# First cross attention: four passes of eight batches turned into one run over 32 batches

## What is computed

```python
def _L0_xattn_ref(x, context, Wq, Wk, Wv, Wo, bo):      # x (32,128,128), context (32,77,96)
    q = (x @ Wq).reshape(B, S, 8, 64).transpose(0, 2, 1, 3)
    k = (context @ Wk).reshape(B, 77, 8, 64).transpose(0, 2, 1, 3)
    v = (context @ Wv).reshape(B, 77, 8, 64).transpose(0, 2, 1, 3)
    attn = softmax(einsum('bhsd,bhld->bhsl', q, k) * 64 ** -0.5)
    out = einsum('bhsl,bhld->bhsd', attn, v)
    return out.transpose(0, 2, 1, 3).reshape(B, S, 512) @ Wo + bo
...
x = _layernorm(x + _L0_xattn_ref(x, ctx_768, ...), axis=-1)
```

## Time and profile before

| | us |
|---|---|
| runs shown | 3458.25, 3458.6, 3462.52 |
| median | 3458.6 |
| the profiled execution | 3463.82 |
| its span | 3462.0 |
| first cross attention in it, to the next stage's first instruction | 269.45 (7.8% of the span) |

### The profile page before, as it was taken

The page is one execution under the profiler, slowest core; times in us unless marked ns, Lnnn a source line. Parts: engine busy times, 40 slices in busy tenths (PEclk is TensorE's granted clock), DMA queues, the critical chain, the costliest instruction groups (busy, mean ns, idle before and its releaser), DMA issues. The chain is left out here.

```text
span 3462.0 us, 84257 instructions
## 1 busy us (share of the span) xinstructions
PE 2679.9 (77%) x31931; PEld 1923.7 (56%) x31931; DVE 2379.6 (69%) x7057; ACT 1979.8 (57%) x3723; POOL 1688.9 (49%) x1265
## 2 busy tenths in 40 slices
PE   1899999888857678889799999866655657858846
PEld 1677777656647565566355555544333447845546
DVE  6678778756557878956667766559973544568945
ACT  1688888644436746755555555555423724556747
POOL 3788888422257615510356656613321257805544
PEclk9999999899958887999999999977768858978958
DMA  4333333221112301000000000000007012301013
GB/s 136 63 63 61 60 62 62 43 95 51 51 40 75 97 1 69 2 1 1 1 3 2 3 3 2 3 1 19 25 22 231 7 46 66 92 15 38 2 34 102
DMA packets 103292, 151.42 MB, mean 44 GB/s; under 512 B 26266, under 2 KB 76524, under 8 KB 101756
## 3 DMA queue, kind: packets, MB, share of 16 engines
q1 hardware_dynamic: 91418, 122.93, 14.3%
q0 software_dynamic: 10912, 22.70, 2.0%
q10 hardware_dynamic: 562, 0.41, 0.1%
HBM read 81.20 MB, written 49.04 MB: 38 GB/s over the span
## 5 line engine op out<-in xcount | busy, mean ns | idle before, releaser
L551 DVE TENSOR_REDUCE MX<-banks 128x8 f32<-128x1152 f32 x128 | 173.8, 1358 | 97.4 <-PE banks L320 97.3
L2550 POOL TENSOR_TENSOR SM<-SM,RZ 128x1232 f32<-128x1232 f32 x64 | 144.0, 2250 | 160.3 <-DVE RZ L2592 160.3
L1810 POOL DMA_INDIRECT sorted_rows<-SRC,IDX x160 | 156.8, 980 | 131.8 <-DVE IDX L1939 85.1
L1823 POOL DMA_INDIRECT expert_results<-Y,DST x181 | 178.4, 986 | 81.1 <-DVE DST L2006 34.4
L1592 PE MATMUL banks<-XC,WR 128*128 128x128 f32 x1448 | 197.7, 281 | 0.5 <-ACT XC L1712 0.4
L514 POOL TENSOR_TENSOR FL<-FL,sb_f_sin 128x1024 f32<-128x1024 f32 x60 | 142.3, 2371 | 83.3 <-DMA FL<-RAW 83.2
L1592 PEld LDWEIGHTS banks<-XC,WR 128*128 128x128 f32 x1448 | 181.1, 197 | 2.7 <-ACT XC L1712 2.1
L2889 POOL TENSOR_TENSOR KQ<-T,EX 128x1024 f32<-128x1024 f32 x32 | 76.2, 2381 | 209.2 <-ACT EX L2870 209.2
L555 DVE TENSOR_TENSOR SM<-banks,MX 128x512 f32<-128x512 f32 x256 | 168.2, 678 | 0.0
L461 ACT COPY PT<-banks 128x1024 f32<-128x1024 f32 x128 | 128.4, 1004 | 54.3 <-PE banks L346 54.3
L2518 ACT COPY PT<-banks 128x1024 f32<-128x1024 f32 x128 | 129.0, 1008 | 48.4 <-PE banks L2439 47.6
(11 more groups left out here) (579 smaller groups left out, 8774.7 us busy)
## 6 DMA issues: line engine op xcount, KB each, us to landing
FL<-RAW SPq DMA_DIRECT2D x508, 64.0 KB, 2.3
sorted_rows<-in_zeros_dram SPq DMA_DIRECT2D x33, 528.0 KB, 8.2
XR<-sorted_rows SPq DMA_DIRECT2D x181, 66.0 KB, 1.9
SRC<-expert_results SPq DMA_DIRECT2D x16, 512.0 KB, 6.9
T<-s4d_k_dram SPq DMA_DIRECT2D x8, 1024.0 KB, 10.4
weight_region<-in_l_ffn__wall_dram SPq DMA_DIRECT2D x1, 4112.0 KB
film_dram<-F SPq DMA_DIRECT2D x8, 512.0 KB, 2.9
FO<-film_dram SPq DMA_DIRECT2D x8, 512.0 KB, 4.2
```

Source lines behind the costliest of these rows:

```text
L551: nc.vector.tensor_reduce(MX[:, n % 2], sc, AXX, ALU.max).then_inc(s.mx, 1)
L1810: nc.gpsimd.indirect_dma_start(out=rows, out_offset=bass.IndirectOffsetOnAxis(ap=IDX[:, k, t:t + 1], axis=0), in_=SRC[:, t, k, :], in_offs ...
L1823: nc.gpsimd.indirect_dma_start(out=results, out_offset=bass.IndirectOffsetOnAxis(ap=DST[:, j % ST:j % ST + 1], axis=0), in_=Y[:, j % ST, : ...
L2550: nc.gpsimd.tensor_tensor(SM[:, t % 4], SM[:, t % 4], bc(RZ[:, t % 2, :].unsqueeze(2), [P, H, L]), ALU.mult).then_inc(s.nm, 1)
```

## The change

`l0_xattn` becomes one run over `NB` = 32 batches in eight groups of four; `decoder` calls it once, with all transfers in one list. In detail:

- The projections of group 0 for `x`, keys and queries stand ahead of the loop; its values, and the units of every later group, are spread over the steps of the group before (`SLOTS`: three places in each step, 13 units a group). They use two banks (2 and 3) in turn. A unit waits until the unit two places ahead has been copied out. ACT copies `x`, the queries and two of four values, DVE the keys and the other values.
- `XT`, `QT`, `KT`, `VA` hold two groups instead of eight batches.
- Scores: eight matmuls of 64 rows and 77 columns instead of four of 128 rows and 154 columns; the keys lose their zeros and the clearing. Even heads go to bank 0, odd heads to bank 1. There is one pair of banks instead of two, so that the scores of a batch wait for the subtraction of the batch before.
- The weights are turned by halves: 16 transposes of 64 rows instead of 8 of 128, into two banks, and ACT copies them once instead of twice. `SM` has 51 more columns so that each transpose is 128 wide.
- The layer norm is taken for each batch, by the logarithm and the exponential on ACT (three short instructions), a product on DVE, and scale and shift on ACT, four and more steps behind the batch. No table is changed in the loop.
- POOL adds the bias to four batches at a time, in place, and no longer clears the weights.
- `E.r` and `E.xt` go.

```diff
-    proj = [("k", g, j) for g in range(NG) for j in range(NJ)] + [("q", g, j) for g in range(NG) for j in range(NJ)] + \
-           [("v", t, 0) for t in range(NB)]
+    NB = B_ALL
+    GROUP = ["X", "K0", "K1", "K2", "K3", "Q0", "Q1", "Q2", "Q3", "V0", "V1", "V2", "V3"]
+    SLOTS = [[["X"], ["K0", "K1"], ["K2"]], [["K3"], ["Q0"], ["Q1"]], [["Q2"], ["Q3"], ["V0"]], [["V1"], ["V2"], ["V3"]]]
+    def due(i, slot):
...
+        new = [(item, i // GB + 1) for item in SLOTS[i % GB][slot]] if i // GB + 1 < NG else []
+        first = [[("V0", 0), ("V1", 0)], [("V2", 0)], [("V3", 0)]][slot] if i == 0 else []
+        return first + new
...
             def _(pe):
+                def produce(item, g):
+                    k = place[item, g]
+                    if k >= 2:
+                        taken(pe, *order[k - 2])
...
                 def scores(t):
-                    if t >= 2:
-                        pe.wait_ge(s.sub, t - 1)
+                    if t >= 1:
+                        pe.wait_ge(s.sub, t)
                     for j in range(NJ):
-                        ins = nc.tensor.matmul(PS[:, 2 * (t % 2) + j // 2, j % 2 * 2 * L:(j % 2 + 1) * 2 * L], QT[:, j, t * P:(t + 1) * P],
-                                               KT[:, j, t].rearrange("p o l -> p (o l)"), start=True, stop=True)
+                        for o in range(2):
+                            ins = nc.tensor.matmul(PS[:, o, j * L:(j + 1) * L], QT[HALF[o], g % 2, j, b * P:(b + 1) * P],
+                                                   KT[HALF[o], g % 2, j, b, :], start=True, stop=True)
...
-                        for h in range(4):
-                            ins = nc.tensor.transpose(PS[0:L, 4 + a, h * P:(h + 1) * P], SM[:, t % 3, 4 * a + h, :], E.ident)
+                    for h in range(H):
+                        for r in range(2):
+                            ins = nc.tensor.transpose(turned[:, h, r, :], SM[HALF[r], t % 3, h * L:h * L + P], E.ident[HALF[r], HALF[r]])
...
+                for item in GROUP[:9]:
+                    produce(item, 0)
                 for i in range(NB + 3):
-                    if 2 <= i < NB + 2:
-                        transposes(i - 2)
                     if i < NB:
                         scores(i)
+                    if 2 <= i < NB + 2:
+                        weights_T(i - 2)
+                    for unit in due(i, 0):
+                        produce(*unit)
                     if i >= 3:
                         project(i - 3)
+                    for unit in due(i, 1):
+                        produce(*unit)
                     if 2 <= i < NB + 2:
                         mix(i - 2)
+                    for unit in due(i, 2):
+                        produce(*unit)
...
             def _(act):
+                for i in range(NB + 7):
+                    if 2 <= i < NB + 2:
...
+                        nc.scalar.copy(PT[:, t % 2].rearrange("k h (r q) -> k h r q", r=2), turned).then_inc(s.pt, 1)
                     if i < NB:
                         act.wait_ge(s.sub, i + 1)
+                        nc.scalar.activation(heads(i), heads(i), ACT.Exp, scale=float(D) ** -0.5).then_inc(s.ex, 1)
+                    for unit in due(i, 0) + due(i, 1):
+                        take(*unit)
+                    if 2 <= i < NB + 2:
...
+                        nc.scalar.copy(ZT[:, t % 2, :], z_bank).then_inc(s.zt, 1)
+                    for unit in due(i, 2):
+                        take(*unit)
+                    if 5 <= i < NB + 5:
+                        act_ln_rstd_one(nc, act, E, s, i - 5)
+                    if i >= 7:
+                        act_ln_apply_one(nc, act, E, s, i - 7, XB[:, i - 7, :], E.x[:, i - 7, :])
...
             def _(dve):
+                for i in range(NB + 7):
...
+                    for unit in due(i, 0):
+                        take(*unit)
+                    if 1 <= i <= NB:
+                        total(i - 1)
+                    for unit in due(i, 1):
+                        take(*unit)
+                    if 3 <= i < NB + 3:
+                        t = i - 3
+                        dve.wait_ge(s.o_ps, t + 1)
+                        dve.wait_ge(s.rb, t // GB + 1)
+                        nc.vector.tensor_tensor(XB[:, t, :], o_bank, XB[:, t, :], ALU.add).then_inc(s.res, 1)
+                    if 4 <= i < NB + 4:
+                        dve.wait_ge(s.res, i - 3)
+                        dve_ln_stats_one(nc, dve, E, s, i - 4, XB[:, i - 4, :])
+                    if 6 <= i < NB + 6:
+                        dve_ln_shift_one(nc, dve, E, s, i - 6)
+                    for unit in due(i, 2):
+                        take(*unit)
...
-        chunks("a", ("l0_xattn", l0_xattn, lambda i: {"prefetch": (list(l1_cross) if i == 0 else []) + clean[i::PASSES]}))
+        run("l0_xattn", l0_xattn, prefetch=list(l1_cross) + clean)
```

More of the change, by code:

```diff
@@ new lines, in due @@
+    def due(i, slot):
+        if i >= NB:
+            return []
+        new = [(item, i // GB + 1) for item in SLOTS[i % GB][slot]] if i // GB + 1 < NG else []
+        first = [[("V0", 0), ("V1", 0)], [("V2", 0)], [("V3", 0)]][slot] if i == 0 else []
+        return first + new
+    order = [(item, 0) for item in GROUP[:9]] + [unit for i in range(NB) for slot in range(3) for unit in due(i, slot)]
+    place = {unit: k for k, unit in enumerate(order)}
+    with sublayer(nc, "u_ps x_in k_in q_in va_in vd_in one pad rb s_ps mx sub ex sm rz nm pt_ps pt z_ps zt o_ps res w_ld" + LN) as (s, ctx):
@@ L622, in l0_xattn @@
[L622 to L633, removed]
@@ L635, in done, with bank_of, heads @@
-        def done(eng, u):
-            if u % 2 == 0:
-                eng.wait_ge(s.ua, u // 2 + 1)
+        XB = E.x
+        HALF = (slice(0, 64), slice(64, 128))
+        sc = PS[:, 0:2, 0:NJ * L].rearrange("p o (j l) -> p o j l", l=L)
+        turned = PS[:, 4:6, :].rearrange("k r (h q) -> k h r q", q=64)
+        z_bank, o_bank = PS[:, 6, :], PS[:, 7, 0:P]
+        def bank_of(item, g):
+            return PS[:, 2 + place[item, g] % 2, :]
+        def heads(t):
+            return SM[:, t % 3, 0:H * L].rearrange("p (h l) -> p h l", l=L)
@@ L687, in mix @@
                 def mix(t):
+                    g, b = t // GB, t % GB
+                    pe.wait_ge(s.pt, t + 1)
+                    taken(pe, f"V{b}", g)
                     if t >= 1:
                         pe.wait_ge(s.zt, t)
[L690 to L694, removed]
@@ L695, in mix @@
-                    ins.then_inc(s.zt_ps, 1)
+                    for j in range(NJ):
+                        for o in range(2):
+                            h = 2 * j + o
+                            ins = nc.tensor.matmul(z_bank[HALF[o], j * P:(j + 1) * P], VA[:, g % 2, b, h * D:(h + 1) * D],
+                                                   PT[:, t % 2, NJ * o + j, :], start=True, stop=True)
+                    ins.then_inc(s.z_ps, 1)
                 def project(t):
@@ new lines, in take @@
+                def take(item, g):
+                    n = int(item[1:] or 0)
+                    bank = bank_of(item, g)
+                    if item == "X":
+                        act.wait_ge(s.u_ps, place[item, g] + 1)
+                        if g >= 2:
+                            act.wait_ge(s.u_ps, place["Q3", g - 2] + 1)
+                        nc.scalar.copy(XT[:, g % 2, :], bank).then_inc(s.x_in, 1)
+                    elif item[0] == "Q":
+                        act.wait_ge(s.u_ps, place[item, g] + 1)
+                        if g >= 2:
+                            act.wait_ge(s.s_ps, GB * (g - 1))
+                        nc.scalar.copy(QT[:, g % 2, n, :], bank).then_inc(s.q_in, 1)
+                    elif item[0] == "V" and n % 2:
+                        act.wait_ge(s.u_ps, place[item, g] + 1)
+                        if g == 0:
+                            act.wait_ge(s.one, 1)
+                        if g >= 2:
+                            act.wait_ge(s.z_ps, GB * (g - 2) + n + 1)
+                        nc.scalar.copy(VA[0:L, g % 2, n, :], bank[0:L]).then_inc(s.va_in, 1)
@@ new lines, in total @@
+                def total(t):
+                    dve.wait_ge(s.ex, t + 1)
+                    nc.vector.tensor_reduce(SU[:, t % 2, :], heads(t), AXX, ALU.add).then_inc(s.sm, 1)
+                    dve.wait_ge(s.sm, t + 1)
+                    if t >= 2:
+                        dve.wait_ge(s.nm, t - 1)
+                    nc.vector.reciprocal(RZ[:, t % 2, :], SU[:, t % 2, :]).then_inc(s.rz, 1)
+                for item in GROUP[:9]:
+                    take(item, 0)
+                for i in range(NB + 7):
```

182 lines of the change are left out of this document (76 added, 106 removed).

## The result

| | before | changed kernel |
|---|---|---|
| median of the runs | 3460.6 us (4 runs, 3458.3 to 3468.9) | 3408.5 us (4 runs, 3402.5 to 3414.9) |
| ratio, 95% interval | | 0.9838 [0.9816, 0.9859] |
| profiled execution, its span | 3463.8, 3462.0 us | 3408.5, 3406.7 us |
| the stage, from the end of the first self attention | 269.45 us | 215.68 us |

The forecast was 3404 us, from a median of 3458.6 before (3460.6 with a fourth run), and a stage of 214.8. The profiled execution is 55.3 us shorter, of which 53.8 lie in this stage. The table of stretches of the changed kernel cuts the stage as the forecast's sum did: ahead of the loop, steps 0 to 3, the 24 steps with units (started as 719.01 to 871.12), steps 28 to 30, and what follows the last scores. The columns are those of the earlier trace rows.

The account below looks back on a forecast made before the run. PE's work bounds the loop; outside, PE waits in four fills and drains. Head and first steps 32.6, groups 151.8, steps 28 to 30 11.6, tail 14, plus dips and hand-over: 214.8 for 269.45, hence 3404 us, range 3392 to 3418.

Parts of the forecast that it names:

- last scores to last scale: Tail after the last scores: softmax, division, turn, copies, output, layer norm, hand-overs and older scalings, 14 us.
- dips of the clock: TensorE's granted clock falling at times during the stage: about 8 us of 200 possible, 4 taken.
- T: PE's turning of the weights in each step, as 16 half-row transposes: 0.65 us.
- O: PE's output projection matmuls in each step, same instructions as before: 0.98 us.
- S: PE's score matmuls in each step, on halves of the array: 0.72 us, range 0.53 to 1.05.
- M: PE's matmuls on the turned weights in each step, between T and O, unchanged: 1.04 us.
- K1's wait: In each group's first step, the second key unit waits for ACT's copy of turned x behind the exponential: 0.55 us.
- Rival 2: Tile shape changes on PE cost 0.42 us four times a step: 34 us more, 3438; chance 0.16.
- Rival 4: TensorE's clock drops to half for much of the stage: slower, 3498 at half of the work; chance 0.05.
- rival 1: Everything on PE is cheaper: S at 0.53, free tile changes, x's wait hidden, no dips: 3380; chance 0.13.
- rival 3: The two unit banks become the chain, each of 13 units waiting 0.55 us: 46 us more, 3450; chance 0.08.
- rival 5: Transfers or something at the stage's closing barrier give the gain back: same time; chance 0.02.

Follow-up runs that it names:

- the run with all changes together: Changed kernel plus x copied before the exponential, no units between M and scores, idle banks for first units, tail statistics before next residual: 3401.8 us, 0.981 of before.

## Why the forecast was right, step by step

| term | forecast | measured |
|---|---|---|
| ahead of the loop | 8.6 | 10.1 |
| steps 0 to 3 | 7.55, 3.95, 6.05, 6.4 | 8.03, 4.30, 5.76, 6.35 |
| a group, six of them | 25.3, 151.8 | 25.35, 152.1 |
| steps 28 to 30 | 11.6 | 11.7 |
| last scores to last scale | 14 | 16.6 |
| dips of the clock | 4 | 0 behind the head |
| to the next stage | 0.8 | 0.7 |
| **stage** | **214.8** | **215.7** |

**The bound was named rightly.** PE sets the pace of the loop: full-row turning adds to the step what it adds to T, a shorter O shortens the step, a doubled division does nothing to it. And the four heads, fills and drains were the larger part, 39 of 54 us, with the low clock at their starts in it.

**The step's terms were off and met in the sum.** S was taken at 0.72 and is 0.95: 0.92 a group too little. That is near the end of the range at which halves don't run side by side, but they do; the mistake was the price of 0.85 ns a moving column, by which 8 pairs of 77 columns would take 0.53. A pair takes 0.11, as much as a record of O with 128 columns (0.89 / 8), and no less with 64. Against it T is 0.59, not 0.65, O 0.89, not 0.98, M 1.02 to 1.03, not 1.04 (rows 3 themselves give 1.03): 0.66 too much. That these meet within 0.3 a group is luck; so is it that the 1.5 us by which the head and the 2.6 by which the tail came out longer stand against the 4 for dips that did not come. K1's wait was placed exactly (forecast for X's copy 4.0 after S, K1 starts at 4.07); taking it away gave 0.73, not 0.55.

**Changes of tile shape cost less than taken.** Against the forecast's 0.86 for a query or value unit and 0.52 for a key unit, a unit in front of M is 0.09 to 0.20 longer, in front of S 0.15 to 0.20, behind T 0.06 to 0.11. A group holds 25.35 - 13.82 (S, T, O, M) - 9.4 (the units as forecast) - 0.63 (the gap between K0 and K1) = 1.5 us of it, forecast 1.8. Taking one of four changes out gave 0.175 a step. Rival 2 (0.42 each) is out: the 0.42 of the earlier trace rows is what the weight load waits, and it lies beside matmuls that are in the record until 1382.30, after the load has begun. The Trainium skill's rule that a change of mode drains the engine ("TensorEngine Tiling (Array Packing)", Key Properties) agrees with this in so far as the changes that could be priced cost 0.06 to 0.20 us; that each one drains the engine is not shown.

**The clock.** The forecast spread dips over the loop; the rows have the low clock in one place. The table of stretches and PE's timeline of the changed kernel's start:

```profile
684.46:690.70 6.24, 6.21 (x14) 3.76 (x15) 1.91 (x4) 1.86 (x2) 4.90 (x3) 0.50 0.50 146
```

```profile
684.50 1.09 PE L59 MATMUL banks<-sb_c_ident,x_res 128*128 128x128 f32 x4 [2.94 <-PEq L48]
685.37 4.46 PE L683 MATMUL banks<-ctx_T,weight_region 96*128 96x308 f32 x8
689.63 4.27 PE L688 MATMUL banks<-XT,weight_region 128*128 128x512 f32 x8
```

From 684.46 to 690.70 the granted clock is 0.50, 1.2 GHz, with PE busy throughout, so that the four key units take 689.63 - 685.37 = 4.26 us, twice what was taken. The clock had fallen before the stage began: from 673.9 to 684.46, in the drain of the self attention, it is 0.50 with PE busy for 4.9 of 10.6 us. Behind the first scores it is 1.00 until 899. The head paid for the low clock beyond the turning of X, which alone had been priced at it, and the loop paid nothing of its 4 us. Rival 4 had no ground here, and the changed kernel meets the low level less than the one before did.

**The tail was walked as if the queues were empty.** The last division was due at 888.1 and POOL ends it at 890.1. DVE's last sum and what stands ahead of it, the division of the batch before on POOL, the last turn and its copy:

```profile
886.66 1.21 POOL L819 TENSOR_TENSOR SM<-SM,RZ 128x616 f32<-128x616 f32 x1 [2.58 <-DVE RZ L847]
887.08 0.81 DVE L166 TENSOR_TENSOR ln_std<-ln_stats,ln_rstd 128x1 f32<-128x1 f32 x1
887.81 0.78 DVE L843 TENSOR_REDUCE SU<-SM 128x8 f32<-128x616 f32 x1
...
890.76 0.71 PE L713 MATMUL banks<-sb_c_ident,SM 64*128 64x64 f32 x16
...
892.19 0.99 ACT L788 COPY PT<-banks 128x1024 f32<-128x1024 f32 x1
```

The last exponential is done at 886.5, where the walk has 885.9. The last sum stands on DVE behind the layer norm shift of an older batch (L166), a product of one element a row, which here takes 0.81 us. It does not wait for ScalarE, whose part was done at 884.0. It begins 0.42 us into POOL's division of the batch before and ends 0.02 behind it, at 887.89. Of the 32 shifts of the stage 15 begin within a division: all of them take 0.80 or 0.81 and end 0.01 to 0.02 behind it, and the other 17 take 0.12 to 0.16. In the run with each division twice some begin later in a division, take 0.59 or 0.31, and end at the same place. The last turn waits for M of the batch before. That is 0.6, 1.3 and 0.6 us, about the 2.6 by which 14 was short; the turn's copy waits another 0.7, until 892.19, for an older batch's scale, but 1.0 had been taken for such, and what is left behind the turn evens out. In the tail of the run with all changes together one reordering gave 0.5 us, where about 1 was expected.

**Rivals 1, 3 and 5.** Of rival 1 only the missing dips came: S is not 0.53, changes of shape have a price, X's wait is there. In the loop no unit but K1 waits for a bank, and the stage's end gives nothing back: outside the stage the two profiles differ by 1.6 us.

## What to carry to other kernels

A stage that runs in passes pays its head, fill and drain for each; look at the timeline of one pass, subtract the steady steps, and the rest times the number of passes is what one stretch can win. In the steady part take the busiest engine's start-to-start times, also for the price of a neighbour (a unit in front of S, one in front of O), since the label of idle time on TensorE understated it here (0.46 us against 0.73). And where TensorE leads, move what frees its banks ahead of what nobody waits for, as X ahead of the exponential, which was worth 4.4 us in the stage where its labels add up to 2.8. Before a difference between two profiles is put down to an edit, look whether the granted clock at the start was low for as long in both.

## What the runs showed of the hardware

Matmuls and transposes on 64 rows gain by standing near some on the other 64 in the order: scores and turning of a step take 1.54 us with the halves in turn and 2.04 with the halves in a row, and the gain is there even across two lines of code with different work. On its half a record of S follows the one before by 0.11 us and one of T by 0.06, in either order. The time of S doesn't move with 64 or 77 moving columns. A weight load of 64 rows by 128 columns takes 188 ns for S's matmuls and 138 for T's transposes, at the same granted clock of 1.00. A short VectorE instruction that multiplies two tiles of the on-chip memory took 0.81 us instead of 0.13 when it began 0.42 us into GpSimd's division, and ended with it; a statistics instruction that reads one tile took its 0.28 us beside the same division.
